# Context tiles of a gated cross-attention block on 128 rows of PE, and the context keys copied from PSUM by DVE

## What is computed

```python
kvx = einsum('bsi,oi->bso', cond, w_kv_x)          # cond: (8, 64, 256)
kx, vx = split(kvx, 2, axis=-1)
kx = ln(kx.reshape(b, 64, 8, 128), kxln_w, kxln_b)
vx = vx.reshape(b, 64, 8, 128)
xout = gqa(qx, kx, vx)                             # softmax(qx kx^T / sqrt(128)) vx
catq = div_clamp_fp8(concat([core, xout]), proj_smooth)
out = einsum('bsi,oi->bso', catq, wproj) * (proj_in_scale * proj_w_scale)
```

## Time and profile before

| | us |
|---|---|
| median of 3 runs | 961.87 (960.19 to 961.93) |
| the profiled execution | 961.15 |
| its span, first to last instruction | 959.3 |
| PE busy | 832.0 (87%) |
| DVE busy | 785.0 (82%) |
| ACT busy | 753.3 (79%) |
| POOL busy | 734.5 (77%) |
| PE weight loads | 625.0 (65%) |

### The profile page before, as it was taken

One profiled execution on the slowest core, in us unless ns is written; L12 is line 12 of the kernel. 1 busy time (PEld: TensorE's weight loads), 2 busy tenths in 40 slices (PEclk: granted clock), 3 DMA queues, 4 the chain that ended last, 5 costly groups with the idle time before them and its releaser, 6 DMA issues.

```text
span 959.3 us, 21100 instructions
## 1 busy us (share of the span) xinstructions
PE 832.0 (87%) x6406; PEld 625.0 (65%) x6406; DVE 785.0 (82%) x1792; ACT 753.3 (79%) x2433; POOL 734.5 (77%) x570
## 2 busy tenths in 40 slices
PE   0377799999999999999999999999998747788795
PEld 0255467777777777777777777778776325566553
DVE  7899888888888888888888889888887886854356
ACT  3377699999999999999999999999997641343331
POOL 4498799889979988997998999899897236444653
PEclk9697799999999999999999999999999779999998
DMA  9421434224323422522342252234228623678963
GB/s 251 126 88 45 100 58 81 56 56 98 61 55 62 97 55 55 102 57 55 67 92 55 55 104 55 55 72 87 55 55 198 174 75 75 147 170 168 191 173 103
DMA packets 226348, 90.64 MB, mean 94 GB/s; under 512 B 202592, under 2 KB 219968, under 8 KB 226304
## 3 DMA queue, kind: packets, MB, share of 16 engines
q1 hardware_dynamic: 218448, 77.78, 36.9%
q0 software_dynamic: 7856, 12.33, 6.3%
HBM read 31.88 MB, written 10.22 MB: 44 GB/s over the span
## 4 chain that ended last, share of the span: by engine, by line
PE 65%; DVE 15%; ACT 7%; issue 5%; DMA 5%; POOL 2%; SPq 1%; DVEq 0%; ACTq 0%; POOLq 0%
PE S L513 11%; PE A L418 8%; PE A L419 8%; PE T L484 6%; PE S L501 5%; PE JB L543 5%; DMA psrc<-w_lo 4%; PE VB L410 3%; PE VB L412 2%; PE VB L411 2%; PE T L534 2%; DVE stage L1128 2%; ACT zq L781 2%; PE T L411 1%; PE T L412 1%
## 5 line engine op out<-in xcount | busy, mean ns | idle before, releaser
L1637 POOL TENSOR_TENSOR rstd<-var,mhalf 128x8 f32<-128x8 f32 (+1 forms) x128 | 191.1, 1508 | 67.2 <-DVE var L1206 66.8
L418 PE MATMUL A<-w_hi,xq 128*128 128x256 f16 (+1 forms) x1024 | 188.1, 250 | 35.6 <-DVE v_lo L1180 21.1
L419 PE MATMUL A<-w_lo,xq 128*128 128x256 f16 (+1 forms) x1024 | 188.0, 250 | 0.0
L1192 DVE TENSOR_SCALAR qT<-T,qmap 128x512 f32<-128x512 f32 x128 | 103.4, 808 | 62.0 <-PE T L484 62.0
L513 PE MATMUL S<-kT,qT 128*128 128x256 f32 x512 | 141.0, 399 | 5.7 <-ACT probx L907 3.4
L1164 DVE TENSOR_REDUCE nmx<-S 128x2 f32<-128x512 f32 (+1 forms) x192 | 114.6, 597 | 23.2 <-PE S L513 23.0
L418 PEld LDWEIGHTS A<-w_hi,xq 128*128 128x128 f16 x1024 | 101.5, 99 | 46.8 <-issue 30.2
L899 ACT ACTIVATE prob<-S,nmx 128x256 f32<-128x256 f32 x256 | 119.6, 485 | 11.2 <-DVE nmx L1164 10.0
L1704 POOL TENSOR_TENSOR raw<-raw,rstd 128x1024 f32<-128x1024 f32 x64 | 126.4, 1975 | 0.0
L1688 POOL TENSOR_TENSOR prob<-prob,rl 128x1024 f32<-128x1024 f32 x64 | 121.0, 1891 | 0.0
L513 PEld LDWEIGHTS S<-kT,qT 128*128 128x128 f32 x512 | 89.5, 193 | 40.1 <-issue 14.1
(11 more groups left out here) (251 smaller groups left out, 2392.1 us busy)
## 6 DMA issues: line engine op xcount, KB each, us to landing
stage<-wallT SPq DMA_DIRECT2D x8, 1024.0 KB, 5.0
yd<-pT SPq DMA_DIRECT2D x46, 128.0 KB
wp<-wpT POOLq DMA_DIRECT2D x1, 2048.0 KB, 30.9
zd<-zr SPq DMA_DIRECT2D x8, 256.0 KB, 2.4
out<-xs SPq DMA_DIRECT2D x8, 256.0 KB, 2.2
xs<-x SPq DMA_DIRECT2D x1, 1792.0 KB, 21.2
raw<-w13T SPq DMA_DIRECT2D x2, 704.0 KB, 4.7
sq<-w13T SPq DMA_DIRECT2D x2, 704.0 KB, 4.4
```

The costliest lines, as they stand in the source:

```text
L418: nc.tensor.matmul(o, l, w_hi[:, c, col:col + n], start=(c == 0), stop=False)
L419: last = nc.tensor.matmul(o, l, w_lo[:, c, col:col + n], start=False, stop=(c == HC - 1))
L1192: nc.vector.tensor_scalar(qT[:, p, k, :, :].rearrange("p h s -> p (h s)"), o[:, :], qmap[:, 2 * k:2 * k + 1], qmap[:, 2 * k + 1:2 * k + 2] ...
L1637: return nc.gpsimd.tensor_tensor(dst, src, mhalf[:, 0:n], ALU.pow)
```

## The change

The low-part product of the context (L534) takes all 128 rows of vx_lo, whose rows 64 to 127 are set to zero once before the first tick; low_vx writes only the 64 upper ones from then on. The transpose of the context keys (L493) takes all 128 rows of `raw` and the whole identity, and writes 128 columns of T1, of which the last 64 are zeros that nobody reads. copy_x moves from ACT, after L932, to DVE, after low_v and ahead of the second maxima; its semaphore a_x becomes d_kx, for which PE's L484 into T0 and POOL's L1711 wait. On DVE it waits for the context projection and for the key transpose of step n-2.

```diff
@@ transpose_q, PE
-                        done(pe, a_x, n); done(pe, d_vx, n)
+                        done(pe, d_kx, n); done(pe, d_vx, n)
@@ transpose_k, PE
-                    nc.tensor.transpose(T1[:, S:KT], raw[0:SC, p, UKX, :], idt[0:SC, 0:SC]).then_inc(mm_kT, 1)
+                    nc.tensor.transpose(T1[:, S:S + P], raw[:, p, UKX, :], idt[:, :]).then_inc(mm_kT, 1)
@@ pv_cross, PE
-                    nc.tensor.matmul(T1[:, :], vx_lo[0:SC, vg, :], both[0:SC], start=False, stop=True).then_inc(mm_xo, 1)
+                    nc.tensor.matmul(T1[:, :], vx_lo[:, vg, :], both, start=False, stop=True).then_inc(mm_xo, 1)
@@ ACT
-                def copy_x(n, p):
-                    done(act, d_vx, n)
-                    done(act, mm_kT, n - 2)
-                    nc.scalar.activation(raw[0:SC, p, UKX, :], T0[0:SC, 0:D], ACT.Copy).then_inc(a_x, 1)
...
-                if live(n0): copy_x(n0, par(0))
@@ DVE
-                    nc.vector.scalar_tensor_tensor(vx_lo[:, g, :], T0[:, D:2 * D], VSCALE / WSCALE, vx_hi[:, g, :], ALU.mult,
+                    nc.vector.scalar_tensor_tensor(vx_lo[0:SC, g, :], T0[0:SC, D:2 * D], VSCALE / WSCALE, vx_hi[0:SC, g, :], ALU.mult,
                                                    ALU.subtract).then_inc(d_vx, 1)
+
+                def copy_x(n, p):
+                    done(dve, mm_x, n)
+                    done(dve, mm_kT, n - 2)
+                    nc.vector.tensor_copy(raw[0:SC, p, UKX, :], T0[0:SC, 0:D]).then_inc(d_kx, 1)
...
                 if live(n0): low_v(n0)
+                if live(n0): copy_x(n0, par(0))
...
             nc.vector.memset(raw[:, :, UKX, :], 0.0)
+            nc.vector.memset(vx_lo[SC:P, :, :], 0.0)
@@ normalise_k, POOL
-                    done(pool, a_x, n)
+                    done(pool, d_kx, n)
```

More of the change, by code:

```diff
@@ L241, in build @@
         ld_pT = [sem("ld_pT0"), sem("ld_pT1")]
[L242 to L245, removed]
+        a_q0, a_sq1, a_q1, a_sqk, a_v, a_vxh, a_kT, a_e0, a_e1, a_ex, a_ph, a_phx, a_core, a_xo = (
+            sem("a_" + n) for n in "q0 sq1 q1 sqk v vxh kT e0 e1 ex ph phx core xo".split())
+        d_v, d_vx, d_ssq, d_ss, d_varq, d_var, d_qT, d_qxT, d_m0, d_m1, d_mx, d_rl, d_pl, d_plx, d_clip, d_cq, d_x1, d_kx = (
+            sem("d_" + n) for n in "v vx ssq ss varq var qT qxT m0 m1 mx rl pl plx clip cq x1 kx".split())
         g_rstdq, g_uq, g_rstd, g_u, g_normx, g_norm = (sem("g_" + n) for n in "rstdq uq rstd u normx norm".split())
@@ L661, in rank @@
                     pe.wait_ge(ld_rows, 32)
-                    done(pe, d_qxT, STEPS - 1); done(pe, a_x, STEPS - 1)
+                    done(pe, d_qxT, STEPS - 1); done(pe, d_kx, STEPS - 1)
                 def o(a, b):
```

## The result

The change made the kernel slower: 968.87 us, median of 5 runs (965.18 to 971.54), against 960.19 (956.54 to 961.93) for the kernel before. The ratio is 1.0094, with a 95% interval of 1.0065 to 1.0123. Forecast were 955.6 and a range up to 959.8. The profiled execution of after took 965.18 with a span of 963.3; that of before 961.15 with 959.3. In the changed kernel the ACT lines have moved up by 5 or 6, the DVE lines by 1 to 6 and the POOL lines down by one: ACT's scaled outputs are L927, its exponentials L894 and kT L883, DVE's read_q is L1191, the copy L1185, the maxima L1158, low_v L1174, and POOL's are L1638 (roots), L1705, L1645.

What follows compares the result with a forecast made beforehand. PE was taken as the bound, with ACT's kT and POOL as near floors. From the profiled 961.15, 5.5 for seven batches and 0.7 for start and end leave 954.9; with 0.7 for the median, 955.6 us, range 949.5 to 959.8.

Steps and rivals of the forecast that it cites:

- ACT gains 0.16 a tick: Moving copy_x off ACT frees 0.16 us of its queue each tick; only the front tick shows it.
- rival 4: DVE's copy waits for POOL's L1704, making the maxima and ACT late: 41 us slower, about 1000 us; chance 0.05.
- PE's price of a 64-row tile: On PE, 128 rows give back 0.30 us at L534 (0.09 + 0.10 + 0.10) and 0.20 at L493, each tick.
- kT as the bound of L493: PE, earlier by 0.20 us at L493, would wait for ACT's kT at L513, so only 0.015 counts.
- margin of "0.02 to 0.05": Before L513, ACT's kT was said to come at most 0.02 to 0.05 us before it would hold PE.
- The plain tick: A plain tick of the attention loop goes from 10.23 to about 9.915 us, 0.315 less.
- The batch: Each batch of 8 ticks loses 0.79 us, since ticks bound by POOL keep their length; seven batches give 5.5 us.
- rival 2: Another phase between POOL and DVE shortens POOL's floor, 0.2 us in 22 ticks: 4.4 us more, 951.2; chance 0.15.
- The mark of 82.3 for a refuted floor: A batch under 82.3 us would refute POOL as the second floor of the loop; 82.9 was expected.
- The copy on DVE: The copy takes 0.28 us and fills DVE's 0.51 us of idle time before the second maxima, so it is free.
- Start and end: Memset, first batch, last ticks and drain together change the time by -2 to +1.5 us, taken as -0.7.
- The "PE switches": A part of the start-and-end sum: 0.3 us given back by PE in the last three ticks.

Runs made afterwards that it cites:

- run 1: The changed kernel with 20 more already-true waits (10 instructions) of ACT before its first tick: 993.46 us, ratio to before 1.0366.
- run 5: The changed kernel with 40 more already-true waits (20 instructions) of ACT before its first tick: 950.40 us, ratio to before 0.9919.
- run 9: The changed kernel with 100 more already-true waits (50 instructions) of ACT before its first tick: 968.56 us, ratio to before 1.0102.
- run 6: The kernel before with 60 more already-true waits (30 instructions) of ACT before its first tick: 985.74 us, ratio 1.0288.
- run 10: The kernel before with only copy_x moved to DVE, plus 40 more waits (20 instructions) of ACT before its first tick: 956.34 us, ratio 0.9984.
- run 7: The kernel before with only L534 on 128 rows, with the zero rows of vx_lo: 952.59 us, ratio 0.9948.
- run 3: The kernel before with both L534 and L493 on 128 rows, copy_x staying on ACT: 951.66 us, ratio 0.9920.
- run 4: The copy alone: the kernel before with only copy_x moved from ACT to DVE, 64-row tiles kept: 987.65 us, ratio 1.0287.

## Why the prediction was wrong

**The step that failed** is "ACT gains 0.16 a tick" with no cost beside it: of the removal of copy_x from ACT the prediction reckoned the time of the instruction and not that ACT's program becomes 14 instructions shorter ahead of the loop and 16 in it. The runs show in its place six stops of ACT, 3.0 us each at the seam, 18 us in all, against 8.7 us that the batches gain. None of the rivals has it; rival 4, the only one with a slower kernel, is another mechanism. Runs 1, 5 and 9 move the changed kernel alone between 993, 950 and 969 us by that length, and runs 6 and 10 do the same to its neighbours, so the cause is shown, not argued. What would have warned: the row of q14 on the page, whose 22 packets show that something is fetched block by block. Only 4 of them fall between 160 and 730 us, so the loop ran nearly without fetches (in after 35 of 51 fall there). ACT's 373 instructions a round against blocks of 128 leave 11 places of room in three. That the edge would be crossed could not be read from the trace of before alone, since c and the 128 come from the later runs. But it could have stood as a rival, with no upper price, since none of its rows has a fetch that stops an engine.

**PE's price of a 64-row tile: right.** In after the middle of a plain tick is, beside the earlier trace rows, PE and then the load of L513:

```profile
458.63 0.27 PE L493 MATMUL T<-idt,raw 128*128 128x128 f32 x1
...
460.12 1.13 PE L513 MATMUL S<-kT,qT 128*128 128x256 f32 x4
461.09 0.38 PE L533 MATMUL T<-pT,vx_hi 128*128 128x512 f16 x1
461.30 0.38 PE L534 MATMUL T<-pT,vx_lo 128*128 128x512 f16 x1
461.52 1.03 PE L513 MATMUL S<-kT,qT 128*128 128x256 f32 x4
...
460.12 0.73 PEld L513 LDWEIGHTS S<-kT,qT 128*128 128x128 f32 x4 [0.41 <-ACT kT L883]
```

L534 follows L533 by 0.21 and is followed after 0.22 (0.31 and 0.32 before), and the four matmuls of the second L513 have 1.03 (1.13 before). The first L513 now has the 1.13, since its load waits for kT. For the three terms 0.09 + 0.10 + 0.10 the run of L534 alone gives 0.30.

**kT as the bound of L493: right.** PE's first L513 now waits for kT (50 times, 22.2 us), and L493 by itself brings 0.02 a tick where 0.015 was worked out. The wait is 0.41 in these ticks, where the prediction named 0.18: it left out the 0.21 that the load waited already (10.9 us in 51 times). So the margin of "0.02 to 0.05" was none: PE's load already waited for kT in before.

**The plain tick: right.** 9.91 where 9.915 was reckoned, in after and in run 5.

**The batch: the mechanism right, the size too small.** Reckoned 0.79; run 5 gives 83.66 - 82.43 = 1.23. The 0.44 more is POOL's. The prediction held the way from the root of step 0 to the end of the queries of step 1 for fixed, 15.84. It became 412.63 + 1.89 - 398.90 = 15.62. Of POOL's instructions in between one changed, the second half of the token normalisation. In before it is

```profile
411.17 1.33 POOL L1644 TENSOR_TENSOR z<-z,rs 128x512 f32<-128x512 f32 x1
```

and in run 5, with the queries behind it,

```profile
408.96 1.11 POOL L1645 TENSOR_TENSOR z<-z,rs 128x512 f32<-128x512 f32 x1
...
412.63 1.89 POOL L1705 TENSOR_TENSOR raw<-raw,rstd 128x1024 f32<-128x1024 f32 x1
```

0.22 less, and again 0.21 after step 5 (1.32 and 1.11): 0.43 a batch. That is rival 2's mechanism, another phase between POOL and its neighbours, but in L1644 and not in the roots. The roots of step 7 stayed at 3.51. Which neighbour it is was not varied; run 7 shows that L534 on 128 rows brings it by itself. The mark of 82.3 for a refuted floor was not reached. The prediction had 0.15 for this case. Without the stops the kernel gains 8.4 us (run 5, 950.40 against 958.79 for before beside it), which lies midway between the 6.3 of the forecast and the 10.7 of rival 2.

**The copy on DVE: right.** The rows of after beside the earlier trace rows:

```profile
461.90 0.47 DVE L1174 SCALAR_TENSOR_TENSOR v_lo<-A,vscale,v_hi 128x256 f16<-128x256 f32 x1
462.29 0.27 DVE L1185 COPY raw<-T 64x128 f32<-64x128 f32 x1
462.58 0.69 DVE L1158 TENSOR_REDUCE nmx<-S 128x2 f32<-128x512 f32 x1
```

0.27 where 0.28 was taken, and the 0.51 us of idle time before the maxima are gone. Its whole worth shows between run 3 and run 5: 951.66 and 950.40, batches of 82.53 and 82.43. That is 0.10 in the front tick, in run 10 too, where 0.16 was reckoned. Rival 4, a copy that POOL blocks, is out: all 64 copies last 0.270 to 0.275.

**Start and end: the wrong sign at the start, the end not told apart.** The memset takes 0.48, the low end of its range. L493 of step 8 starts at 160.6 to 161.6 in the profiled executions of the six kernels with it (160.6 in after, 161.3 in run 5) and at 159.1 to 160.4 in those of the six without (160.2 in before). So the first batch ends about 1.3 us later on the mean, where the prediction took -0.7 for start and end together. The "PE switches" of that sum are the 0.30 around L534; that a switch is what takes it no run shows. With L534 on 128 rows (run 7) the last two ticks up to L493 of step 8 are 10.17 and 9.92 where before has 10.23 and 10.23, and the one ahead of them is 12.04 against 11.69. The part behind the last L493 lasts 219.3 us in after, 224.6 in before, 226.7 in run 5 and 221.8 in run 3, in single executions; the change does not touch it, and a term of 0.7 us can't be seen in it.

**What stays open.** Why the granted clock falls behind a stop at all six returns of the copy alone and of run 1, at five of six in before with 30 instructions, and at none in after and run 9. PE idles 2.45 us at a stop of the copy alone and 2.49 at one of after, and 2.51 at the return of run 6 that keeps the clock, so neither the length of this idle time nor the kernel alone decides it; what else PE does around it was not varied. Also open is which neighbour shortens L1644, and how many blocks ACT holds beyond the estimate of four, since no loop of another length was run.

## What to carry to other kernels

Before an instruction is added to or taken from an engine with a loop, count what the engine executes ahead of the loop and in a round, waits included, and look at the packets of its instruction queue: one more block across the loop can cost more at every return than the edit gives (here 3.0 us against 1.24 a batch). Such a count tells how much room there is only once the place of the loop in its blocks is known; two or three runs with waits ahead of it find it. When a kernel gets slower by a stop with "issue" at the first instruction of a round, shift the loop by waits that are true already and measure again before the edit is judged; here that turned +0.9% into -0.8%. And a neighbour's fixed time is only fixed in its present phase: bound it by the shortest row that the same instruction has in the loop (1.11 for L1644 stood in before).

## What the hardware showed that was not expected

- A return of ACT's loop costs nothing with 373 instructions in three 8 KB blocks, 2.75 us (2.9 with the start of the next operation) with 357 in four, and 2.75 + 2.46 when a block's edge lies right behind the first instruction of the loop. Counted from the branch, the sequencer goes on after 0.2 us in the first case and after 3.6 to 3.7 us in the others.
- Behind a return with a stop five packets of 8 KB come in the round: two at the return and one about each time that ACT enters a new block, one more than the loop has blocks.
- So the shorter loop was the slower one. DVE's loop with 238 instructions in before and 254 in after and POOL's with 94 showed no stop in any run: at every return DVE's next record starts 0.29 to 0.34 us behind the branch, POOL's 0.15.
- A stop of 2.45 us on PE was followed by a granted clock of 0.57 over 4 us in one kernel, and one of 2.49 us by a full clock in another. In run 6 both happened in the same kernel, after 2.46 and 2.51 us. In run 1 PE idles for 4.92 us, and the windows of 4 us from 410 to 422 us show 0.77, 0.50 and 0.87 (columns as in run 4):

```profile
410.00:414.00 4.00, 0.00 (x0) 0.00 (x0) 0.00 (x0) 0.69 (x2) 1.09 (x1) 0.77 0.43 113
414.00:418.00 4.00, 3.80 (x26) 3.37 (x27) 2.12 (x3) 2.84 (x8) 0.00 (x0) 0.50 0.00 0
418.00:422.00 4.00, 4.00 (x25) 3.17 (x24) 3.23 (x8) 3.63 (x14) 2.53 (x2) 0.87 0.00 0
```
